# Order of partitions in three kinds of DMA of a four-stage convolution kernel, and its copies by way of DRAM cut into seven

## The chip, the core and the metric

One core of a Trainium2 chip runs the whole kernel. The metric is the device time of one launch in microseconds. The kernel before took 13218.9 us (median of 3 runs, 13193.93 to 13242.16).

## The reference

The input x is 16 images of 32 channels of 64 x 64. Four stages follow one another, each reading a normalised x and adding its result to x:

```
x = x + L0(gn(x))   # Winograd convolution 3x3, 32 -> 32 channels
x = x + L1(gn(x))   # offsets = prelu(conv3x3(x)); at 9 taps a pixel, sample x bilinearly at the tap + offset,
                    # out[o] = sum over taps and 4 channels of the group: w * sample
x = x + L2(gn(x))   # four 3x3 convolutions with weights +-scale, a 1x1 one, rounded to integers between
x = x + L3(gn(x))   # 3x3 convolution and |row difference| x W_edge, times a squeeze-and-excite gate
```

L1, the deformable convolution, is the costly one: each of the 9 taps of each of 4096 pixels is sampled at its own place.

## The kernel before, in words

**Layout.** An image is held as 128 partitions: 4 strips of 16 rows times 32 channels. The 16 images go through a software pipeline: in period n the kernel does for image n+1 stages L0, the offsets of L1 and their tables (the code's `a`), for image n the sampling and convolution of L1 (`b`), and for image n-1 stages L2 and L3 (`c`). A period has 24 slots (`SLOTS`); every engine runs through the same slots in the same order, with semaphores between them. There are 18 periods (-1 to 16), of which periods 0 to 15 hold the sampling.

**The sampling.** Six of the nine taps are fetched by GpSimd with indirect DMAs from a table in DRAM, 192 per image (L580). The other three, the dense taps, are computed. In each slot TensorE multiplies an image of 64 rows by 12 columns (twice, for two windows, so 128 partitions) by a matrix `select` that holds for each sample the weight of each row: 3 tiles `t` of 3 matmuls of 512 columns (L1328, two instructions each, so 18). VectorE multiplies each tile by the column weights `col_hat` (L1069), and TensorE sums the result with `w_dense` (L1340, `fold_dense`). `select` is made by ScalarE from `row_in` with an Abs (L630) and a Relu (L632).

**The dense loads.** For each slot, `row_in` and `col_hat` are each 128 partitions of 1536 numbers (768 KB), read from one row of a small table in DRAM, `coord_table`. `row_in` holds two different rows of 1536 numbers, each repeated for 64 partitions, and ScalarE's queue issues it (`load_rows`, L620). `col_hat` holds four, each repeated for 32 partitions, and SyncE issues it (`load_cols`, L437). Both are double buffered. In slot s ScalarE makes `select` for slot s+1 and then issues the load of `row_in` for slot s+2; SyncE issues `col_hat` for slot s+1 as soon as TensorE has folded slot s-1.

**The copies by way of DRAM.** The 3 x 3 convolutions want the image as 96 partitions: 3 horizontal shifts times 32 channels, whole rows. `store_plane` (L394) writes the 128 strip partitions to a plane of 32 channels in DRAM, and `load_taps` (L399) reads it back three times, shifted by one element. There are six such pairs per period: one for the offsets and five for L2 and L3. Each is placed in the slots so that the load is issued one slot after the store and the convolution comes one slot after the load.

**Order of SyncE's queue.** SyncE issues nearly all DMAs, in slot order, and each waits for its own semaphore first. The store of the image table, two times three DMAs in slots 18 and 19 (L457, L458, L460), stands in the same queue; so do the store of the coordinate table (L501, slot 21) and the load of the next image from it (L447). At the end of a period ScalarE's load of `row_in` for the next image (issued in slot 22) waits for the coordinate table, which VectorE computes in slot 21 (L1042 to L1053).

## Time and profile before

| | |
|---|---|
| runs, median (lowest to highest) | 13218.9 us (13193.93 to 13242.16) |
| profiled execution | 13156.62 us |
| its span | 13154.8 us |
| TensorE busy | 5385.4 us (41%), mean granted clock 0.679 |
| VectorE busy | 2994.6 us (23%) |
| ScalarE busy | 1772.0 us (13%) |
| GpSimd busy | 3027.3 us (23%) |
| DMA | 1049.75 MB, mean 80 GB/s, 16 engines |

The page's second part shows a flat picture over the whole span: TensorE 3 to 4 tenths, DMA 2 tenths, every engine idle more than half of the time. The chain of waits says what the span consists of; the share of busy time does not. A "slot" below is one step of the 24 of a period; in the middle of the trace a period takes about 793 us.

### The profile page before, as it was taken

To read this page: it belongs to the slowest core of one execution; us is meant where nothing else is said; L and a number is where in the kernel's file an instruction comes from. 1 tells how busy PE (TensorE), PEld (TensorE's weight loads), DVE (VectorE), ACT (ScalarE), POOL (GpSimd) and SP (SyncE) were. 2 spreads that over 40 slices of the span, in tenths; PEclk is the share of its full clock that TensorE was granted. 3 is DMA by queue.
4 is the path that set the end of the run, shared out by engine and by line. 5 is a ranking of instruction groups with operands and counts; after the bars stand their busy time and mean duration, and the time that the engine had idled before them with its cause. 6 is when DMAs were issued, how large, how long until landed. Compare 5 with 4: busy or idle time off the path is not lost.

```text
span 13154.8 us, 73595 instructions
## 1 busy us (share of the span) xinstructions
PE 5385.4 (41%) x24993; PEld 2557.4 (19%) x24993; DVE 2994.6 (23%) x5550; ACT 1772.0 (13%) x1990; POOL 3027.3 (23%) x3095
## 2 busy tenths in 40 slices
PE   2444344443444434434443434434344443344432
PEld 1222112121221212112121211211122121121110
DVE  2222122222222222222222222212222222222111
ACT  1111111111111111111111111111111111111110
POOL 2222132221222222122221322213222222222210
PEclk7666676666666666666666766666666666666665
DMA  3222222222222222222222222222222222222221
GB/s 86 74 85 76 73 92 77 82 81 77 86 77 92 79 80 83 77 85 80 88 76 74 91 77 84 80 75 87 76 88 79 81 79 78 90 78 80 80 74 37
DMA packets 447808, 1049.75 MB, mean 80 GB/s; under 512 B 237844, under 2 KB 274036, under 8 KB 438260
## 3 DMA queue, kind: packets, MB, share of 16 engines
q1 hardware_dynamic: 299252, 541.60, 12.8%
q10 hardware_dynamic: 49920, 301.99, 5.9%
q0 software_dynamic: 98304, 201.52, 5.7%
q8 instruction: 233, 3.82, 0.1%
q14 instruction: 99, 0.81, 0.0%
HBM read 943.72 MB, written 99.59 MB: 79 GB/s over the span
## 4 chain that ended last, share of the span: by engine, by line
DMA 71%; another core or an unknown queue 12%; SPq 8%; ACT 4%; DVE 1%; PE 1%; issue 1%; ACTq 0%; DVEq 0%
DMA row_in<-coord_table 64%; SPq L458 6%; ACT select L630 4%; DMA col_hat<-coord_table 3%; DMA plane_c<-xn_c 2%; SPq L460 1%; DMA coord_table<-wino 1%; PE ps_r L1328 1%; DMA taps_c<-plane_c 1%; DMA taps_c<-plane_act 0%; SPq L501 0%; DMA wino<-plane_a 0%; ACTq L620 0%; DVE wino L1048 0%
## 5 line engine op out<-in xcount | busy, mean ns | idle before, releaser
L580 POOL DMA_INDIRECT ring<-patch_table,idx_part x3072 | 3018.5, 983 | 9678.9 <-ACT idx_part L608 6132.5
L1328 PE MATMUL ps_r<-select,image 128*128 128x512 f32 x6912 | 3741.3, 696 | 2668.3 <-DVE col_hat L1069 1645.1
L1069 DVE TENSOR_TENSOR col_hat<-ps_r,col_hat 128x512 f32<-128x512 f32 x1152 | 794.9, 690 | 6990.5 <-PE ps_r L1328 4088.1
L1328 PEld LDWEIGHTS ps_r<-select,image 128*128 128x128 f32 x6912 | 1485.3, 225 | 4570.1 <-issue 2580.8
L630 ACT ACTIVATE select<-row_in,minus_row 128x1536 f32<-128x1536 f32 x384 | 604.6, 1575 | 10293.5 <-DMA row_in<-coord_table 10293.5
L1340 PE MATMUL ps_y<-col_hat,w_dense 128*32 128x128 f32 x9216 | 491.3, 362 | 914.1 <-ACT conv_out L656 903.5
L1354 PE MATMUL ps_t<-ident,values 128*128 128x128 f32 x1024 | 203.3, 333 | 1403.2 <-ACT samples L649 1403.1
L632 ACT ACTIVATE select<-select,one_col 128x1536 f32<-128x1536 f32 x384 | 604.6, 1574 | 12.5
L1340 PEld LDWEIGHTS ps_y<-col_hat,w_dense 128*32 128x32 f32 x9216 | 321.0, 144 | 1121.0 <-ACT conv_out L656 961.7
L1080 DVE TENSOR_TENSOR ring<-ring,w_cur 128x768 f32<-128x768 f32 x512 | 486.0, 949 | 17.6 <-DMA ring<-patch_table,idx_part 17.6
L1354 PEld LDWEIGHTS ps_t<-ident,values 128*128 128x128 f32 x1024 | 154.0, 174 | 1597.2 <-ACT samples L649 1486.5
L1271 PE MATMUL ps_a<-wino,w_freq 128*128 128x64 f32 x1152 | 218.2, 376 | 389.4 <-ACT wino L666 362.9
L1124 DVE TENSOR_SCALAR work_c<-work_c 128x1024 f32<-128x1024 f32 x64 | 44.4, 694 | 1262.6 <-ACT work_c L707 1262.2
L1314 PE MATMUL ps_c<-taps_c,w_edge_conv 96*32 96x512 f32 x768 | 134.2, 852 | 480.1 <-DMA taps_c<-plane_c 480.1
L1314 PE MATMUL ps_c<-taps_c,w_sign 96*32 96x512 f32 x768 | 125.8, 823 | 487.6 <-DMA taps_c<-plane_c 487.6
L1271 PEld LDWEIGHTS ps_a<-wino,w_freq 128*128 128x128 f32 x1152 | 217.5, 291 | 403.4 <-ACT wino L666 365.0
L1314 PE MATMUL ps_a<-wino,w_off 96*32 96x512 f32 x768 | 126.1, 825 | 409.6 <-DMA wino<-plane_a 409.6
L1084 DVE TENSOR_TENSOR ring<-ring 128x384 f32<-128x384 f32 x512 | 281.7, 550 | 4.4
L1314 PE MATMUL ps_c<-taps_c,w_signs 96*32 96x512 bf16 x1152 | 131.9, 627 | 316.4 <-DMA taps_c<-plane_act 316.4
L649 ACT COPY samples<-ps_t 128x512 f32<-128x512 f32 x256 | 147.6, 576 | 421.9 <-PE ps_t L1354 421.9
L1090 DVE TENSOR_TENSOR values<-ring 128x192 f32<-128x192 f32 x512 | 179.4, 350 | 4.5
L1282 PE MATMUL ps_a<-ident,wino_c 128*128 128x128 f32 x128 | 30.6, 418 | 316.6 <-ACT wino_c L684 316.6
(225 smaller groups left out, 2628.0 us busy)
## 6 DMA issues: line engine op xcount, KB each, us to landing
row_in<-coord_table ACTq DMA_DIRECT2D x384, 768.0 KB
col_hat<-coord_table SPq DMA_DIRECT2D x384, 768.0 KB
taps_c<-plane_c SPq DMA_DIRECT2D x32, 1608.8 KB
ring<-patch_table,idx_part POOLq DMA_INDIRECT x3072, 3.7
taps_c<-plane_act SPq DMA_DIRECT2D x48, 804.4 KB
wino<-plane_a SPq DMA_DIRECT2D x16, 1608.8 KB
plane_c<-xn_c SPq DMA_DIRECT2D x32, 520.0 KB
coord_table<-wino SPq DMA_DIRECT2D x64, 216.0 KB
```

The lines of the kernel that those rows point to most:

```text
L458: sp.dma_start(to[0:P - XW, lo:hi, 2 * C:], stage[XW:P, lo:hi]).then_inc(table_out, 16)
L580: nc.gpsimd.indirect_dma_start(out=ring[j][:, h % 2, k, :], out_offset=None, in_=table, in_offset=bass.IndirectOffsetOnAxis(ap=idx_part[:, ...
L630: nc.scalar.activation(sel, row_in[s % 2][:], ACT.Abs, bias=minus_row[:]).then_inc(row_in_read, 1)
L632: nc.scalar.activation(sel, sel, ACT.Relu, bias=one_col[:], scale=-1.0).then_inc(select_made, 1)
L1069: v.tensor_tensor(hat_t, ps_r[:, (s + t) % 2], hat_t, ALU.mult).then_inc(tile_weighed, 1)
L1080: return chain.add(v.tensor_tensor(tile, tile, wts, ALU.mult))
L1084: return chain.add(v.tensor_tensor(tile[:, :, 0:2 * C], tile[:, :, 0:2 * C], tile[:, :, 2 * C:], ALU.add))
L1271: ins = mm(ps_a[:, f % 2, b_ * NT:(b_ + 1) * NT], flat_w(w_freq, f * FREQ + b_), wino_v[:, f, :, b_, :], start=True, stop=True)
L1314: ins = mm(ps[s * C:(s + 1) * C, h], w[:, k0 + dy], src[:, r0:r0 + RS // 2, 0:W], start=(dy == 0), stop=(last and dy == 2))
L1328: ins = mm(ps_r[:, (s + t) % 2], image[:, m, t], select[s % 2][:, m], start=(m == 0), stop=(m == PAIRS - 1))
L1340: ins = mm(ps_y[j * C:(j + 1) * C, :], w_dense[:, DT - 1 - e].rearrange("p g o -> p (g o)"), col_hat[s % 2][:, t, j * P:(j + 1) * P], star ...
L1354: ins = nc.tensor.transpose(ps_t[:, j * P:(j + 1) * P], values[:, g % 2, j, 4 * k:4 * k + 4].rearrange("p k c -> p (k c)"), ident[:])
```

## The change

Four DMAs change their access patterns.

- `row_in`: the partitions are ordered as 64 image rows times 2 windows (partition = 2 x row + window) and no longer 2 x 64. The DRAM side of the load is then 64 (repeated) x 2 x 1536, not 2 x 64 (repeated) x 1536.
- `col_hat`: 32 x 4 instead of 4 x 32, in the same way.
- `store_plane`: four DMAs of 32 partitions instead of one whose pattern is 4 x 32.
- `load_taps`: three DMAs of 32 partitions instead of one whose pattern is 3 x 32.

All else follows from the new partition order: the image is loaded to every second partition, ScalarE's copy of it (`place_image`, three per period) reorders columns from (w, c) to (c, w), the weights `w_dense` get a mask of 16 partitions per group and a raw copy of their own, and `minus_row` is minus half the partition number, rounded. These last are done once, ahead of the loop. The counts that are waited for grow with the number of DMAs.

```diff
             def store_plane(dst, src, done):
-                sp.dma_start(dst.ap()[:, 1 + XW:1 + XW + STRIPS * RS * XW].rearrange("c (s x) -> s c x", s=STRIPS),
-                             src[:, 1 + XW:1 + XW + RS * XW]).then_inc(done, 16)
+                for s in range(STRIPS):
+                    sp.dma_start(dst.ap()[:, 1 + XW + s * RS * XW:1 + XW + (s + 1) * RS * XW],
+                                 src[s * C:(s + 1) * C, 1 + XW:1 + XW + RS * XW]).then_inc(done, 16)
             def load_taps(dst, plane, done):
-                sp.dma_start(dst, bass.AP(plane, 0, [[1, SHIFTS], [XG + 2, C], [1, XG]])).then_inc(done, 16)
+                for dx in range(SHIFTS):
+                    sp.dma_start(dst[dx * C:(dx + 1) * C, :], plane.ap()[:, dx:dx + XG]).then_inc(done, 16)
...
-                             part.rearrange("o (w x) -> (o w) x", w=WQ)[:, None, :].to_broadcast([WQ, C, WT * HALF])
+                             part.rearrange("o (w x) -> o w x", w=WQ).to_broadcast([C, WQ, WT * HALF])
                              ).then_inc(col_hat_in[s % 2], 16)
...
-                        sp.dma_start(image_next[h * H:(h + 1) * H, m * WIN * C:(m + 1) * WIN * C].rearrange(
+                        sp.dma_start(image_next[h:P:2, m * WIN * C:(m + 1) * WIN * C].rearrange(
...
-                    sp.wait_ge(plane_a_out, n * 16 + 16)
+                    sp.wait_ge(plane_a_out, n * PLANE_OUT + PLANE_OUT)
...
-                                    part.rearrange("o (h x) -> (o h) x", h=2)[:, None, :].to_broadcast([2, H, PAIRS * HALF])
+                                    part.rearrange("o (h x) -> o h x", h=2).to_broadcast([H, 2, PAIRS * HALF])
                                     ).then_inc(row_in_in[s % 2], 16)
...
-                new = image_next.rearrange("p (m t f) -> p m t f", m=PAIRS, t=WT)
+                new = image_next.rearrange("p (m t w c) -> p m t c w", m=PAIRS, t=WT, w=WQ)
...
-                    nc.scalar.copy(image[:, :, t], new[:, :, t]).then_inc(image_ready, 1)
+                    nc.scalar.copy(image[:, :, t].rearrange("p m (c w) -> p m c w", w=WQ), new[:, :, t]).then_inc(image_ready, 1)
...
-TAPS_IN = 16
+PLANE_OUT = STRIPS * 16
+TAPS_IN = SHIFTS * 16
```

On SyncE's queue, in slots 2 to 5 of the loop's body, before (`plane_c` and `plane_act` are the planes in DRAM, `xn_c` and `act_c` the strips, `taps_c` the 96 partitions; register instructions stand as ISA and REGISTER_ALU):

```order
L394 DMA plane_c<-xn_c 4x32x1040
L434 ISA
L437 ISA
L437 DMA col_hat<-coord_table 128x1x1536
L471 ISA
L399 DMA taps_c<-plane_c 96x1x4290
L434 ISA
L437 ISA
L437 DMA col_hat<-coord_table 128x1x1536
```

and now:

```order
L397 DMA plane_c<-xn_c 32x1040 x4
L439 ISA
L442 ISA
L442 DMA col_hat<-coord_table 128x1x1536
L476 ISA
L403 DMA taps_c<-plane_c 32x4290 x3
L439 ISA
L442 ISA
L442 DMA col_hat<-coord_table 128x1x1536
```

Nothing has changed its place: the store and the load of each copy stand where they stood, as four and three instructions in a row. The loads of `col_hat` (here) and of `row_in` (on ScalarE's queue) read word for word as before, since only the order inside their patterns differs. TensorE's order has no change but line numbers.

## Rows read from the trace of the kernel before

**Rows 1.** Page, part 4: shares of the chain that ended last, by line.
```profile
DMA row_in<-coord_table 64%; SPq L458 6%; ACT select L630 4%; DMA col_hat<-coord_table 3%; DMA plane_c<-xn_c 2%; SPq L460 1%; DMA coord_table<-wino 1%; PE ps_r L1328 1%; DMA taps_c<-plane_c 1%; DMA taps_c<-plane_act 0%; SPq L501 0%; DMA wino<-plane_a 0%; ACTq L620 0%; DVE wino L1048 0%
```
**Rows 2.** Waits: who waited for whom, us in total, times, longest.
```profile
ACT select L630 <- DMA row_in<-coord_table: 10293.5, 384, 62.3
...
DVE col_hat L1069 <- DMA col_hat<-coord_table: 2901.9, 128, 63.9
```
**Rows 3.** Chain of waits, mid-trace: start us, us, what.
```profile
6003.07 1.58 ACT select L630
...
6004.83 17.49 DMA row_in<-coord_table
...
6024.19 28.66 DMA row_in<-coord_table
```
**Rows 4.** Page, part 3: ScalarE's DMA queue; packets, MB, share of 16 engines.
```profile
q10 hardware_dynamic: 49920, 301.99, 5.9%
```
**Rows 5.** DMA issues with time to landing: whole trace, then 12890 to 13155 us.
```profile
patch_table<-values SPq DMA_DIRECT2D x1, 4224.0 KB, 16.8
...
out<-work_c SPq DMA_DIRECT2D x8, 128.0 KB, 2.2
```
**Rows 6.** Chain of waits at the start and in the last period.
```profile
85.50 39.67 DMA wino<-plane_a
...
12906.56 10.31 DMA plane_c<-xn_c
12916.89 40.32 DMA taps_c<-plane_c
...
12970.51 6.12 DMA plane_act<-act_c
12976.66 19.40 DMA taps_c<-plane_act
```
**Rows 7.** Timeline of SyncE, a store of the image table in mid-trace.
```profile
6381.74 52.37 SPq L458 DMA_DIRECT2D patch_table<-stage  x1
```
**Rows 8.** Page, part 5: the costliest groups on GpSimd and TensorE.
```profile
L580 POOL DMA_INDIRECT ring<-patch_table,idx_part x3072 | 3018.5, 983 | 9678.9 <-ACT idx_part L608 6132.5
L1328 PE MATMUL ps_r<-select,image 128*128 128x512 f32 x6912 | 3741.3, 696 | 2668.3 <-DVE col_hat L1069 1645.1
```
**Rows 9.** Windows: stretch, us, busy PE, PEld, DVE, ACT, POOL, PEclk, DMA share, GB/s.
```profile
5590.00:6383.00 793.00, 336.35 (x1562) 159.44 (x1562) 186.13 (x343) 108.85 (x124) 187.49 (x192) 0.68 0.25 81
...
5650.00:5700.00 50.00, 23.65 (x94) 10.39 (x94) 14.05 (x34) 3.40 (x3) 38.10 (x39) 0.73 0.45 129
...
6017.00:6029.00 12.00, 10.55 (x59) 4.48 (x52) 10.39 (x15) 3.86 (x5) 2.01 (x2) 0.93 0.15 43
...
12896.00:13155.00 259.00, 33.44 (x235) 11.55 (x233) 39.68 (x57) 15.32 (x24) 0.00 (x0) 0.54 0.12 34
```
**Rows 10.** Timeline of a slot that has its loads (start, us, engine, line).
```profile
6017.69 5.95 PE L1328 MATMUL ps_r<-select,image 128*128 128x512 f32 x12
...
6024.87 2.84 PE L1328 MATMUL ps_r<-select,image 128*128 128x512 f32 x6 [1.24 <-DVE col_hat L1069]
...
6027.65 0.64 PE L1340 MATMUL ps_y<-col_hat,w_dense 128*32 128x128 f32 x16
...
6028.86 5.42 PE L1328 MATMUL ps_r<-select,image 128*128 128x512 f32 x12
```
**Rows 11.** Timeline around slot 22, where the coordinate table is awaited.
```profile
6470.40 0.93 DVE L1042 TENSOR_SCALAR wino<-wino 96x128 f32<-96x128 f32 x6
6470.63 5.42 PE L1328 MATMUL ps_r<-select,image 128*128 128x512 f32 x12
...
6486.31 0.25 ACT L733 ACTIVATE hidden<-ps_c,b_att 4x1 f32<-4x1 f32 x1 [9.17 <-DMA coord_table<-wino]
```
**Rows 12.** Timeline of SyncE at the start: four DMAs of 32 partitions in a row.
```profile
2.58 1.81 SPq L384 DMA_DIRECT2D x<-x  x4
```
**Rows 13.** Lines L394 and L399: duration of an issue, ns, min/median/max.
```profile
L394 SPq DMA_DIRECT2D plane_c<-xn_c x32: 549/579/596, 1002.2 to 13085.3; - x32
...
L399 SPq DMA_DIRECT2D taps_c<-plane_c x32: 723/736/783, 1018.2 to 13095.6; - x32
```

More of the change, by code:

```diff
@@ L362, in build @@
         raw_d = raw_part(TAPS * 4)
+        raw_dense = raw_part(TAPS * 4)
         raw_2t = raw_part(CONVS * 3 * C)
@@ L370, in build @@
         prep_small = raw_part(32)
+        dense_mask = raw_part(8)
         n_weight_dmas = 0
@@ L423, in load_later @@
                 sp.dma_start(b_att1[:], batt1).then_inc(weights_in, 16)
+                sp.dma_start(raw_dense, w1d[:, None, :].to_broadcast([C, WQ, TAPS * 4])).then_inc(weights_in, 16)
                 sp.dma_start(raw_2t[0:TAPC, :], w2t).then_inc(weights_in, 16)
                 sp.dma_start(raw_3t[0:TAPC, :], w3t).then_inc(weights_in, 16)
-            n_weight_dmas = STRIPS * (len(later) + 1) + 3
+            n_weight_dmas = STRIPS * (len(later) + 1) + 4
             def load_cols(n, s):
@@ L470, in c_taps @@
                     i = at.index(s)
-                    sp.wait_ge(plane_c_out, n * (16 * len(at)) + 16 * (i + 1))
+                    sp.wait_ge(plane_c_out, n * (PLANE_OUT * len(at)) + PLANE_OUT * (i + 1))
                     if i in (0, len(at) - 1):
@@ L558, in _ @@
                                           channel_multiplier=1, allow_small_or_imprecise_dtypes=True))
-                chain.step(nc.gpsimd.iota(minus_row[ps], pattern=[[0, 1]], base=0, channel_multiplier=-1,
-                                          allow_small_or_imprecise_dtypes=True))
+            chain.step(nc.gpsimd.iota(minus_row[:], pattern=[[0, 1]], base=0, channel_multiplier=-1,
+                                      allow_small_or_imprecise_dtypes=True))
             chain.step(nc.gpsimd.memset(one_col[:], 1.0))
@@ L781, in prepare_rest @@
                 chain.step(v.tensor_scalar(group_mask[:], group_mask[:], float(STRIPS), None, ALU.mult))
+                chain.step(v.tensor_reduce(dense_mask, ident[:].rearrange("p (g i) -> p g i", i=4 * WQ), AX.X, ALU.add))
                 dve.wait_ge(weights_in, 16 * n_weight_dmas)
@@ L791, in prepare_rest @@
                     chain.add(v.tensor_scalar(w_dconv[:, :, g, :], by_chunk, group_mask[:, g:g + 1], None, ALU.mult))
-                    chain.add(v.tensor_scalar(w_dense[:, :, g, :], raw_d4[:, TAPS - DT:TAPS, :], group_mask[:, g:g + 1],
-                                              -1.0, ALU.mult, ALU.mult))
+                    chain.add(v.tensor_scalar(w_dense[:, :, g, :],
+                                              raw_dense.rearrange("p (k o) -> p k o", o=4)[:, TAPS - DT:TAPS, :],
+                                              dense_mask[:, g:g + 1], -1.0, ALU.mult, ALU.mult))
                 signs = raw_2t[0:TAPC, :]
@@ L1225, in _ @@
             dve.wait_ge(grid_ready, 1)
+            chain.step(v.tensor_scalar(minus_row[:], minus_row[:], 0.5, 0.25, ALU.mult, ALU.add))
+            chain.step(v.tensor_scalar(minus_row[:], minus_row[:], ROUND, ROUND, ALU.add, ALU.subtract))
             dve.wait_ge(zeroed, 4)
```

## The prediction

> **What bounds the kernel now.** I read the chain of waits first. Of the span, 64% is the flight of one load, `row_in` [rows 1], and no engine's work reaches 5%. The waits say the same from the engine's side: ScalarE stands 10293.5 us before its Abs for that load, 384 times of 384 [rows 2], 26.8 us each on average; VectorE waits a further 2901.9 us for `col_hat`. The reader should see in the chain how it closes on itself [rows 3]: the Abs of slot s+1 starts, 1.6 us later the load for slot s+2 is issued, and the next Abs starts when that lands. Only one load is in flight at a time, so a slot can't be shorter than load + 1.8 us. The shortest flights are 17.49 us, most are 28 to 40, when other transfers sit on the same DMA engines.
>
> How fast is the load? Its queue moved 301.99 MB in 5.9% of 16 engines' span [rows 4], that is 0.059 x 16 x 13154.8 = 12418 us of engine time, 24.3 GB/s for an engine while it works. One load is 786432 bytes, so 32.4 us of engine time. It lands in 17.49 us at best: that is two engines (16.2 us) and 1.3 us around them. Two is the outermost dimension of its pattern (2 x 64). The copies, with 3 and 4 outside, are slow as well: in the last period nothing else is in flight, and yet the taps take 40.32 us (1608.8 KB, even less than 3 x 24.3 GB/s) and the plane's store 10.31 us [rows 6], while a store of 32 partitions (128 KB) lands in 2.2 us with three more beside it, and a write of 4224 KB whose outermost dimension is 128 in 16.8 us, 257 GB/s [rows 5]. That is more than ten engines at 24.3 GB/s. I read from it that the outermost dimension sets how many engines work, and take all 16 for 32, 64 and 128. So the DMA engines are not full (25% in a period [rows 9]); the kernel waits for the two or three of them that get the work.
>
> The Trainium skill, "DMA: Bandwidth & Descriptors", section "Why a DMA increments its semaphore by 16 and not by 1", says that a DMA is spread over the largest number up to 16 that divides the slowest dimension of both its sides. By that rule the new patterns (64 or 32 outside, 128 or 32 partitions) all get 16 engines; the trace agrees on the two of `row_in`, and no row shows a repeated source with 16.
>
> **The change, part by part.**
>
> *`row_in` and `col_hat`.* With 16 engines a load needs 32.4 / 16 = 2.0 us of transport and 1.3 us around it: 3.3 us at best. `col_hat` is issued at about the same time and uses the same engines, and the gathers too, so I take 5 to 6 us. Bound from above: all 16 engines now read the same 12 KB of DRAM, which no row shows; the fastest 50 us of the trace moved 129 GB/s [rows 9], and at that rate both loads together take 12.2 us. The closed chain then gives 1.8 + 5.5, about 7.5 us a slot (at worst 14). It is 33 us now (793 / 24).
>
> *What is late next.* TensorE. In a slot that has its loads [rows 10] the 18 instructions on the image start 0.43 us apart at full clock, 7.7 us; then VectorE must weigh the third tile before the last fold, and the next slot starts 1.4 us after the last matmul's step: 9.1 us for a slot with nothing else in it. That is above 7.5. I add up TensorE's path over a period:
> - matmuls on the image: 6912 / 16 = 432 x 0.43 = 186 us [rows 8, 10];
> - TensorE's other work: (5385.4 - 3741.3) / 16 = 103 us at the mixed clock of now; 95 us when more of it runs at full clock;
> - the idle moment at each slot's end, 0.4 us x 24 = 10 us;
> - slots where another engine is late. The end of a period is the largest: VectorE starts the coordinates at 6470.40, and ScalarE's next work, behind the wait for their table, comes at 6486.31 [rows 11], while TensorE began that slot at 6470.63 and needs its result before it may fold. The slot becomes 18 us instead of 9, so 9 us, none of it shortened by the change. Behind the heavy VectorE slots (5, 8, 9, 21), where it has 5 to 8 us of L0, L2 and offset work after the third tile and TensorE only allows about 4.5, I count 1 to 4 us each, 17 us in all. Together 26 us;
> - clock and late loads: the granted clock is 0.93 in a stretch where TensorE is busy 10.55 of 12 us and 0.68 over a period where it is busy 42% [rows 9]. I expect it nearly always at 2.4 GHz (level 1.0), and at 1.2 GHz for about a tenth of the image matmuls after a stall: 19 us. Loads that come late behind taps or table stores: 22 us, with nothing but judgement behind it; bounds 0 and 24 x 4 = 96.
>
> Sum: 186 + 95 + 10 + 26 + 41 = 358 us a period against 796 (the middle part of the trace, 163 to 12896 us, is 16 periods).
>
> *The seven DMAs.* Per period there are six stores and six loads, so 6 x 3 + 6 x 2 = 30 DMAs more. They cost SyncE 18 x 0.58 + 12 x 0.74 = 19 us a period of issue [rows 13]; SyncE has nothing to compute, and each copy has one to two slots (15 to 30 us) before it is used. One copy: four issues 2.3 us, 520 KB at 257 GB/s 2.1, around it 1.3: 5.7 us instead of 10.3; the taps three issues 2.2 us, 1608.8 KB 6.4, 1.3: about 9 us (10 if the issues are not overlapped) instead of 40.3. In bf16 5 instead of 6.1 and 6.7 instead of 19.4. Inside a period they are hidden behind TensorE's slots. Queued behind them on SyncE are the loads of `col_hat`, whose slack is a slot of TensorE minus their 5 us; that is where cover may be thin. SyncE's stall at the table store, 52.37 us [rows 7], comes, as I read it, from a DMA queue that is full behind the taps; it should go to the few us that the transfers need.
>
> The Trainium skill speaks against this part: in the same page, "Rules for kernel authors", small transfers are to be merged into one large one, and "Anatomy of one DMA" puts about 2 us of fixed cost on each. If the extra 30 each took 2 us in a row, a period would be 60 us longer, 960 us in all. The trace has four DMAs of 32 partitions issued in 1.81 us [rows 12], and those of the output landing in 2.2 us, so the fixed parts overlap, and I keep only the issue time.
>
> *Ends.* Start: 163 us up to the first `row_in`; the taps' 39.67 us [rows 6] go to 9 and the store saves 5, so 127. Last period: 259 us [rows 9], minus 2 x 31.3 and 3 x 12.9 for taps, 2 x 4.8 and 3 x 1.1 for stores: 145.
>
> *ScalarE's strided copy of the image, the longer setup, two more tiny VectorE instructions:* three copies a period, now 0.5 us; if the order (c, w) doubled them, 1.5 x 16 = 24 us; setup under 5 us. Not counted, in the range.
>
> **The sum.** 16 x 358 + 127 + 145 = 6000 us, against the profiled execution's 13156.62 (span 13154.8). The median of the runs lies 0.5% above that execution, so 6030; I say 6000.
>
> **Rivals.**
> 1. *Transport stays the bound.* 1049.75 MB over 384 slots is 2.73 MB a slot. The 257 GB/s is one lone contiguous write; sources repeated from one small place, small pieces, and reads and writes mixed may give much less, and with engines waiting for one another at the same DRAM or the same partitions the whole may stay near 129 GB/s. Then a slot takes 21 us, and the kernel 384 x 21.2 + 272 = 8400 us. For it: nothing in the trace is both wide and repeated. Against it: two engines reading one place side by side keep 24.3 GB/s each, and 129 was reached without pressure. 7000 to 9500 us.
> 2. *GpSimd's gathers.* 3072 x (0.983 + 0.30) = 3940 us, 246 a period, 31 us for every three slots [rows 8]. The three lightest slots take 31 us too. If denser VectorE work slows each gather's issue by a third, a period comes to about 410 us: 6850 us.
> 3. *The change doesn't do what it says.* If the number of engines hangs on something else than the outermost dimension, both loads keep two and four engines, and the time stays at 13200. Against it stands 17.49 us, which fits two so well.
> 4. *Slower.* One mechanism: 16 engines hammer the same 12 KB of DRAM, and each read queues behind fifteen others. It decides from the point where `row_in` takes over 27 us, which is 16 engines together below 29 GB/s, less than the 45 that two reach now (786432 / 17.49 us). A load of 30 us gives 13.2 + 0.384 x 3 ms, some 14400 us.
>
> **Chances.** Forecast 0.73 (its own range 5500 to 6900), transport 0.17, gathers 0.05, no effect 0.03, slower 0.02. The range that should hold 8 in 10: below, a period of 320 us (no late loads, full clock, VectorE's slots better hidden) gives 5400; above, the 96 us of late loads plus gathers, or the lower part of rival 1, give 7500. A measurement of this kernel tells 0.3% from no change. Faster by more than that 0.95, within 0.03 (rival 3), slower 0.02.
>
> **What would show it.** Right: Abs waits for `row_in` under 6 us in most slots and the chain of waits runs through TensorE, VectorE and the coordinates' table; periods near 358 us; taps of the last period near 9 us; granted clock above 0.9; L458 a few us; DMA near 170 GB/s. Wrong: `row_in` still heads the chain with more than 10 us of flight (rival 1); GpSimd's share above 75% with VectorE waiting for `ring` (rival 2); flights of 17 us unchanged (rival 3). The weakest term is the 41 us of clock and late loads, then the 17 us behind VectorE; each hangs on how the engines' small delays add up.

## The result, and the profile after

The changed kernel takes 5254.25 us (median of 4 runs, 5238.0 to 5263.32) against 13213.41 us: ratio 0.3974, 95% interval 0.3961 to 0.3988. The forecast was 6000 us, with a range of 5400 to 7500. The direction and the cause were right; the time lies 12% below the forecast and 3% below the range. The numbers below are of the profiled execution, with a span of 5261.5 us.

From the page's first four parts: busy time by engine, the granted clock in 40 slices, ScalarE's DMA queue, and the shares of the chain of waits by engine and by line.

```profile
PE 4408.5 (84%) x24993; PEld 2077.6 (39%) x24993; DVE 2987.9 (57%) x5553; ACT 1793.4 (34%) x1990; POOL 3259.5 (62%) x3094
...
PEclk8999989899999999999899899999999999899995
...
q10 hardware_dynamic: 55296, 302.01, 17.2%
...
PE 50%; DMA 22%; DVE 14%; SPq 7%; issue 4%; ACT 2%; ACTq 0%; POOL 0%; DVEq 0%; another core or an unknown queue 0%; POOLq 0%
PE ps_r L1339 33%; DMA taps_c<-plane_c 8%; PE ps_c L1325 6%; DMA wino<-plane_a 4%; DMA plane_a<-xn_a 3%; DMA plane_c<-xn_c 3%; PE ps_a L1282 3%; PE ps_a L1325 2%; PE ps_y L1351 2%; DMA col_hat<-coord_table 2%; SPq L397 2%; DVE col_hat L1077 2%; PE ps_t L1365 1%; SPq L403 1%; SPq L506 1%
```

`row_in` had 64% of the chain of waits [rows 1]; it is no longer among the lines named. TensorE has half of it. DMAs still have 22%, and most of that is the copies. The queue of `row_in` moved the same bytes in 0.172 x 16 x 5261.5 = 14480 us of engine time, so 20.9 GB/s an engine where it was 24.3 [rows 4], 14% less. Sixteen engines on one 12 KB source do not get in one another's way by more than that; how much of the 14% is the shared source, and how much the other transfers that now run beside it, isn't shown.

The number of engines can be read off the packets. A load of `row_in` has 128 packets of 6144 bytes, one for each partition. Before, the queue had 49920 packets [rows 4], 384 x (128 + 2); now it has 55296, 384 x (128 + 16). The trace has the rest as packets of 4 bytes: two a load before and sixteen now, which fits one for each engine at the end of its share. In the last period of the kernel before, the load of taps has three of them and the store of a plane four; now each of the seven DMAs has sixteen.

The waits (engine, line, for whom; us in total, times, longest):

```profile
ACT select L635 <- DMA row_in<-coord_table: 924.9, 143, 22.9
...
DVE col_hat L1077 <- DMA col_hat<-coord_table: 373.4, 55, 14.9
ACT hidden L738 <- DMA coord_table<-wino: 195.7, 14, 14.1
PE ps_c L1325 <- DMA taps_c<-plane_c: 195.0, 32, 17.0
...
PE ps_r L1339 <- DVE col_hat L1077: 153.2, 114, 9.1
PE ps_a L1325 <- DMA wino<-plane_a: 131.5, 16, 14.8
PE ps_c L1418 <- ACT hidden L738: 92.8, 15, 6.7
```

ScalarE's wait for `row_in` fell from 10293.5 to 924.9 us, VectorE's for `col_hat` from 2901.9 to 373.4 [rows 2]. What TensorE itself waits for is now the thing to read, and it is short. The first load of `row_in`, where the forecast's start ends, is issued at 125.58 us:

```profile
125.58 0.66 ACTq L625 DMA_DIRECT2D row_in<-coord_table  x1
```

A slot with nothing but its loads, from the timeline:

```profile
2343.94 7.99 PE L1339 MATMUL ps_r<-select,image 128*128 128x512 f32 x18
...
2346.52 0.57 ACTq L625 DMA_DIRECT2D row_in<-coord_table  x1
...
2353.08 5.42 PE L1339 MATMUL ps_r<-select,image 128*128 128x512 f32 x12
2353.16 1.58 ACT L635 ACTIVATE select<-row_in,minus_row 128x1536 f32<-128x1536 f32 x1 [4.86 <-DMA row_in<-coord_table]
```

The next slot's matmuls begin 9.14 us after this one's: the 9.1 us of the forecast [rows 10]. `row_in` is issued at 2346.52 and its Abs starts at 2353.16, 6.6 us later (17.49 at best before [rows 3]); `select` is double buffered, so TensorE does not feel that. Four stretches of the span (columns as in [rows 9]):

```profile
150.80:418.00 267.20, 247.24 (x1372) 120.38 (x1372) 149.30 (x288) 99.37 (x104) 206.55 (x200) 0.96 0.67 212
418.00:4857.00 4439.00, 3846.17 (x21868) 1808.80 (x21868) 2598.08 (x4800) 1560.57 (x1733) 2850.66 (x2688) 0.94 0.69 206
4857.00:5123.50 266.50, 247.23 (x1343) 111.69 (x1344) 135.42 (x219) 95.79 (x98) 166.32 (x159) 0.96 0.65 204
5123.50:5261.50 138.00, 36.30 (x238) 12.38 (x236) 39.70 (x57) 15.32 (x24) 0.00 (x0) 0.58 0.27 64
```

The first stretch and the third are the first and the last period with sampling, and take 267 us each; the 14 between them take 4439 / 14 = 317 us each. The fourth is the rest of the kernel. The granted clock is 0.94 where it was 0.68 [rows 9], DMA moves 206 GB/s and not 81.

The end of the kernel, from the chain of waits:

```profile
5136.67 2.21 DMA plane_c<-xn_c
5139.70 9.36 DMA taps_c<-plane_c
...
5164.27 1.73 DMA plane_act<-act_c
5166.82 4.68 DMA taps_c<-plane_act
```

These are the flights of the last DMA of each group, counted from its own issue: 9.36 us for the taps instead of 40.32, in bf16 4.68 instead of 19.40, the stores 2.21 instead of 10.31 and 1.73 instead of 6.12 [rows 6]. In the middle of the trace the taps are slower, and TensorE waits for them:

```profile
2674.33 12.50 DMA taps_c<-plane_c
...
2817.36 13.81 DMA wino<-plane_a
```

One such place on TensorE, slot 15, where the offsets' convolution awaits its taps, and the two windows around it:

```profile
2513.38 8.37 PE L1325 MATMUL ps_a<-wino,w_off 96*32 96x512 f32 x48 [10.15 <-DMA wino<-plane_a]
```

```profile
2503.40:2513.30 9.90, 0.00 (x0) 0.00 (x0) 5.47 (x7) 0.00 (x0) 7.91 (x7) 0.62 1.02 228
2513.40:2518.50 5.10, 5.10 (x24) 1.17 (x28) 0.00 (x0) 3.15 (x2) 3.88 (x5) 0.50 0.65 188
2522.40:2530.20 7.80, 7.80 (x22) 3.45 (x20) 2.71 (x4) 0.12 (x1) 0.94 (x1) 1.00 0.38 118
```

While TensorE stands still the DMA engines are full (share 1.02, 228 GB/s): taps, `row_in` and `col_hat` are in flight at once. Behind the wait the first matmuls run at a granted clock of 0.50, the lower level of 1.2 GHz, and only then at 1.00. A wait costs itself and some us more. I add it up from the matmuls' groups (busy us, mean ns, idle before them):

```profile
L1339 PE MATMUL ps_r<-select,image 128*128 128x512 f32 x6912 | 3205.4, 612 | 208.9 <-DVE col_hat L1077 153.2 <-ACT image L646 50.7 <-issue 1.8
...
L1325 PE MATMUL ps_c<-taps_c,w_sign 96*32 96x512 f32 x768 | 128.1, 836 | 125.7 <-DMA taps_c<-plane_c 125.7
L1325 PE MATMUL ps_a<-wino,w_off 96*32 96x512 f32 x768 | 127.8, 835 | 131.5 <-DMA wino<-plane_a 131.5
L1325 PE MATMUL ps_c<-taps_c,w_edge_conv 96*32 96x512 f32 x768 | 118.7, 764 | 69.2 <-DMA taps_c<-plane_c 69.2
...
L1325 PE MATMUL ps_c<-taps_c,w_signs 96*32 96x512 bf16 x1152 | 75.7, 399 | 48.9 <-DMA taps_c<-plane_act 48.9
```

TensorE waits 125.7 + 131.5 + 69.2 + 48.9 = 375.3 us for copies.

### The profile page after: what moved, and what is told of

It is laid out like the page before. It is cut to its first block, busy times and chain, and to the rows that moved or that the text cites. A ratio compares the mean times of both kernels' runs of the same rounds, so it can differ in the third digit from the quotient of the medians.

```text
span 5261.5 us, 74078 instructions
## 1 busy us (share of the span) xinstructions
PE 4408.5 (84%) x24993; PEld 2077.6 (39%) x24993; DVE 2987.9 (57%) x5553; ACT 1793.4 (34%) x1990; POOL 3259.5 (62%) x3094
## 3 DMA queue, kind: packets, MB, share of 16 engines
q10 hardware_dynamic: 55296, 302.01, 17.2%
## 4 chain that ended last, share of the span: by engine, by line
PE 50%; DMA 22%; DVE 14%; SPq 7%; issue 4%; ACT 2%; ACTq 0%; POOL 0%; DVEq 0%; another core or an unknown queue 0%; POOLq 0%
PE ps_r L1339 33%; DMA taps_c<-plane_c 8%; PE ps_c L1325 6%; DMA wino<-plane_a 4%; DMA plane_a<-xn_a 3%; DMA plane_c<-xn_c 3%; PE ps_a L1282 3%; PE ps_a L1325 2%; PE ps_y L1351 2%; DMA col_hat<-coord_table 2%; SPq L397 2%; DVE col_hat L1077 2%; PE ps_t L1365 1%; SPq L403 1%; SPq L506 1%
## 5 line engine op out<-in xcount | busy, mean ns | idle before, releaser
L585 POOL DMA_INDIRECT ring<-patch_table,idx_part x3072 | 3250.8, 1058 | 1810.2 <-issue 1588.7
L1339 PE MATMUL ps_r<-select,image 128*128 128x512 f32 x6912 | 3205.4, 612 | 208.9 <-DVE col_hat L1077 153.2
L1339 PEld LDWEIGHTS ps_r<-select,image 128*128 128x128 f32 x6912 | 1285.4, 194 | 1791.4 <-issue 1496.7
L635 ACT ACTIVATE select<-row_in,minus_row 128x1536 f32<-128x1536 f32 x384 | 605.0, 1575 | 1642.3 <-DMA row_in<-coord_table 924.9
L1351 PE MATMUL ps_y<-col_hat,w_dense 128*32 128x128 f32 x9216 | 367.6, 283 | 23.6 <-DVE col_hat L1077 17.6
L1351 PEld LDWEIGHTS ps_y<-col_hat,w_dense 128*32 128x32 f32 x9216 | 230.1, 111 | 198.1 <-issue 122.4
L1325 PE MATMUL ps_a<-wino,w_off 96*32 96x512 f32 x768 | 127.8, 835 | 131.5 <-DMA wino<-plane_a 131.5
L1325 PE MATMUL ps_c<-taps_c,w_sign 96*32 96x512 f32 x768 | 128.1, 836 | 125.7 <-DMA taps_c<-plane_c 125.7
L1325 PE MATMUL ps_c<-taps_c,w_edge_conv 96*32 96x512 f32 x768 | 118.7, 764 | 69.2 <-DMA taps_c<-plane_c 69.2
L1282 PE MATMUL ps_a<-wino,w_freq 128*128 128x64 f32 x1152 | 139.5, 283 | 26.3 <-DVE wino L892 26.3
L1365 PE MATMUL ps_t<-ident,values 128*128 128x128 f32 x1024 | 153.6, 273 | 0.0
L1282 PEld LDWEIGHTS ps_a<-wino,w_freq 128*128 128x128 f32 x1152 | 139.6, 201 | 33.6 <-DVE wino L892 26.4
L712 ACT ACTIVATE work_c<-ps_c,bn_bias,bn_scale 128x512 f32<-128x512 f32 x160 | 115.4, 771 | 70.6 <-PE ps_c L1325 70.1
L671 ACT COPY wino<-ps_a 128x384 f32<-128x384 f32 x96 | 45.9, 478 | 212.9 <-PE ps_a L1282 212.9
```

What stands on the lines that cost most here:

```text
L585: nc.gpsimd.indirect_dma_start(out=ring[j][:, h % 2, k, :], out_offset=None, in_=table, in_offset=bass.IndirectOffsetOnAxis(ap=idx_part[:, ...
L635: nc.scalar.activation(sel, row_in[s % 2][:], ACT.Abs, bias=minus_row[:]).then_inc(row_in_read, 1)
L1282: ins = mm(ps_a[:, f % 2, b_ * NT:(b_ + 1) * NT], flat_w(w_freq, f * FREQ + b_), wino_v[:, f, :, b_, :], start=True, stop=True)
L1325: ins = mm(ps[s * C:(s + 1) * C, h], w[:, k0 + dy], src[:, r0:r0 + RS // 2, 0:W], start=(dy == 0), stop=(last and dy == 2))
L1339: ins = mm(ps_r[:, (s + t) % 2], image[:, m, t], select[s % 2][:, m], start=(m == 0), stop=(m == PAIRS - 1))
L1351: ins = mm(ps_y[j * C:(j + 1) * C, :], w_dense[:, DT - 1 - e].rearrange("p g o -> p (g o)"), col_hat[s % 2][:, t, j * P:(j + 1) * P], star ...
```

## The experiments

All ratios are to the kernel before, with their 95% interval. Each diff is an excerpt. The time of a slot is the distance between the first image matmul of one slot and of the next, median over the first 15 periods with sampling of a trace.

### The parts apart

`row_only`: the order and the load of `row_in` alone, on the kernel before.

```diff
-   part.rearrange("o (h x) -> (o h) x", h=2)[:, None, :].to_broadcast([2, H, PAIRS * HALF])
+   part.rearrange("o (h x) -> o h x", h=2).to_broadcast([H, 2, PAIRS * HALF])
```

> Of the change only the new order of row_in (64 x 2 outside) and what follows from it; col_hat (4 outside) and the copies (4 and 3 outside) as before. If the outermost dimension sets the number of DMA engines, row_in's flight falls below 10 us, but the lowest three engines still carry all taps and a quarter of col_hat: per period 2.5 MB of taps, 4.7 MB of col_hat, 0.6 MB of stores and about 2 MB of their share of the rest each, near 10 MB at 24.3 GB/s, some 400 to 480 us a period, so 7000 to 8500 us in all, with col_hat and the taps at the head of the waits. Rival, that one closed chain through row_in was all that bound the kernel: under 6000 us.

Measured: 8444.52 us, ratio 0.639 (0.635 to 0.6431), at the upper end of the range. The next wait is the one that the double buffer had hidden; the page's shares of the chain by line:

```profile
DMA col_hat<-coord_table 27%; PE ps_r L1331 11%; DMA taps_c<-plane_c 10%; DMA wino<-plane_a 7%; DMA plane_a<-xn_a 7%; SPq L458 6%; DMA plane_c<-xn_c 5%; DMA plane_act<-act_c 3%; PE ps_c L1317 2%; DMA taps_c<-plane_act 2%; PE ps_a L1317 1%; DVE col_hat L1069 1%; PE ps_a L1274 1%; SPq L447 1%; SPq L501 1%
```

`copies_only`: the seven DMAs alone.

```diff
-   sp.dma_start(dst, bass.AP(plane, 0, [[1, SHIFTS], [XG + 2, C], [1, XG]])).then_inc(done, 16)
+   for dx in range(SHIFTS):
+       sp.dma_start(dst[dx * C:(dx + 1) * C, :], plane.ap()[:, dx:dx + XG]).then_inc(done, 16)
```

> Only the copies in seven DMAs; both dense loads as before. Two engines carry 24 x 393 KB of row_in and 24 x 197 KB of col_hat a period and their share of the rest, about 15.5 MB, 640 us at 24.3 GB/s: 10000 to 11500 us by the theory of engine counts, the chain still headed by row_in. If the copies matter only at start and end of the launch: 13213 - 145 = 13070 us.

Measured: 11906.09 us, 0.901 (0.8953 to 0.9067), above the 10000 to 11500 us of the theory of engine counts, and far below the 13070 of its rival. The copies' gain shows although `row_in` bounds each slot; as I read it, taps and stores on three or four engines were in the way of the two that its load uses. The gain was overrated, and why isn't shown.

`no_row`: `col_hat` and the copies changed, the order and the load of `row_in` as before.

```diff
-   part.rearrange("o (h x) -> o h x", h=2).to_broadcast([H, 2, PAIRS * HALF])
+   part.rearrange("o (h x) -> (o h) x", h=2)[:, None, :].to_broadcast([2, H, PAIRS * HALF])
```

> All of the change but the new order of row_in. Its flight cannot be under 17.5 us (two engines), so the closed chain gives at least 24 x 19.3 = 463 us a period and, with the sixteenths of all other transfers on the same two engines, about 530: 8000 to 9300 us. Rival, all loads share one capacity and the order of row_in alone does little: under 6500 us.

Measured: 10127.82 us, 0.7664 (0.7616 to 0.7712), above my range: with everything else out of the way `row_in` still holds the kernel at 10128 / 384 = 26 us a slot, and has 87% of the chain of waits.

`dense_only`: both dense loads changed, the copies as before, one DMA each.

```diff
-   for dx in range(SHIFTS):
-       sp.dma_start(dst[dx * C:(dx + 1) * C, :], plane.ap()[:, dx:dx + XG]).then_inc(done, 16)
+   sp.dma_start(dst, bass.AP(plane, 0, [[1, SHIFTS], [XG + 2, C], [1, XG]])).then_inc(done, 16)
```

> row_in and col_hat in the new order, the copies by way of DRAM as single DMAs as before. If the copies are exposed where a convolution waits for them: flights of taps of 30 to 45 us instead of 12, in three slots of a period (4, 15, 20) about 25 us more each, a few more behind the three smaller ones and SyncE's table store stalling again: period 318 + 80 to 120 us, 6400 to 7300 us in all. Rival, the prediction's step that the copies lie hidden behind TensorE's slots: only start and last period longer, about 5254 + 145 = 5400 us.

Measured: 7714.81 us, 0.5838 (0.5802 to 0.5875), above the 6400 to 7300 us expected and 2461 us above the changed kernel. TensorE waits for the copies:

```profile
PE ps_c L1323 <- DMA taps_c<-plane_c: 1083.0, 32, 54.5
PE ps_c L1323 <- DMA taps_c<-plane_act: 853.0, 48, 32.7
PE ps_a L1323 <- DMA wino<-plane_a: 574.7, 16, 53.1
```

That is 2511 us against 375 in the changed kernel, and 2136 of the 2450 us between the two spans. The store of the image table shows the full queue again, once behind taps and once (26 us earlier) not, in the timeline of SyncE:

```profile
2239.80 2.80 SPq L461 DMA_DIRECT2D patch_table<-stage  x1
...
2263.73 0.78 SPq L401 DMA_DIRECT2D taps_c<-plane_c  x1
...
2265.36 39.42 SPq L461 DMA_DIRECT2D patch_table<-stage  x1
```

So the 52.37 us [rows 7] were the taps on three engines, as read. The parts don't add: the copies are worth 1307 us alone and 2461 us behind the dense loads; `row_in` is worth 4769 us alone and 4873 us at the end.

### Is it the order of the partitions or the number of engines?

`old_order_split`: the old order of partitions everywhere; `row_in` by 2 DMAs of 64 partitions, `col_hat` by 4 of 32, the copies in seven. Every DMA then has 64 or 32 outermost, too.

```diff
+   for h in range(2):
+       nc.scalar.dma_start(row_in[s % 2][h * H:(h + 1) * H].rearrange("p m x -> p (m x)"),
+                           part[:, h * PAIRS * HALF:(h + 1) * PAIRS * HALF].to_broadcast([H, PAIRS * HALF])
+                           ).then_inc(row_in_in[s % 2], 16)
```

> The partitions in the order of before, but row_in loaded by two DMAs of 64 partitions and col_hat by four of 32, each with its own row as a source; the copies in seven. If only the number that stands outermost in each DMA matters (64 and 32, so all 16 engines), this is as fast as the changed kernel, 5200 to 5350 us, and 384 x 4 more DMAs cost only issue time on queues that have room. Rival: the new order of the partitions, by which neighbours hold different rows, does something of its own (for the DRAM row or the partitions' ports): more than 2% off, either way.

Measured: 5606.2 us, 0.4249 (0.4235 to 0.4262), 6.7% above the changed kernel, so the rival came true. Of the 7959 us gained, 7607 come with any pattern of 32 or 64 outside, and 352 only with the changed kernel's own DMAs. Three ways to lose those 352: one DRAM row read at a time, 64 neighbouring partitions written at a time, or the issue of four more DMAs a slot. For the first two, the next runs take the new order and cut `row_in` in two, first into partitions 0 to 63 and 64 to 127 (both rows in each), then into even and odd ones (one row each).

```diff
+   for h in range(2):
+       nc.scalar.dma_start(row_in[s % 2][h * H:(h + 1) * H].rearrange("p m x -> p (m x)"),
+                           part.rearrange("o (h x) -> o h x", h=2).to_broadcast([H // 2, 2, PAIRS * HALF])
```

```diff
+   for h in range(2):
+       nc.scalar.dma_start(row_in[s % 2][h:P:2].rearrange("p m x -> p (m x)"),
+                           part[:, h * PAIRS * HALF:(h + 1) * PAIRS * HALF].to_broadcast([H, PAIRS * HALF])
```

> The changed kernel with row_in loaded by two DMAs, partitions 0 to 63 and 64 to 127; each still reads two rows in turn (pattern 32 x 2). In the run with the old order and split loads the row_in queue's engines worked at 14.0 GB/s instead of 20.9. If the cause is that one DMA wrote only half of the partitions (two engines at one door to them), this one has the same fault: near 14 to 16 GB/s, and a time between 5254 and 5450 us (col_hat stays as in the changed kernel). If the cause is that all engines read one row of DRAM at a time, this reads two and keeps 20 to 21 GB/s: under 5290 us.

> The changed kernel with row_in loaded by two DMAs, even and odd partitions, so each is spread over all partitions but reads one row of DRAM 64 times. Half of the partitions as the cause: 20 to 21 GB/s kept, under 5290 us. One row of DRAM at a time as the cause: near 14 to 16 GB/s and up to 5450 us. (Against the run before, exactly one of these two should keep its rate.)

Measured: halves 5411.9 us, 0.4092 (0.4074 to 0.4111); evens 5287.44 us, 0.3998 (0.3982 to 0.4015). The queue of `row_in` in the page of the halves, then of the evens:

```profile
q10 hardware_dynamic: 61440, 302.04, 24.0%
```

```profile
q10 hardware_dynamic: 61440, 302.04, 17.2%
```

With spans of 5419.0 and 5282.8 us an engine moves 14.5 GB/s in halves and 20.8 in evens; in one piece it was 20.9. Both use all 16 engines: 61440 packets are 384 x (128 + 2 x 16). So neighbouring partitions slow the engines, a single source row does not. The evens are 0.6% (33 us) slower than the changed kernel, with intervals that overlap, so a second DMA for each `row_in` costs little or nothing. The halves lose 158 us of the 352. The other 194 probably belong to `col_hat`, cut into four DMAs of 32 neighbouring partitions; whether by their place or by their number wasn't tested.

### What the transport still costs

`small_rows` loads 16 of `row_in`'s 1536 numbers from the second image on, `small_taps` 130 of 4290 elements of two of the three f32 taps. Both leave most of a transfer out and keep its place and its waits.

```diff
+   row_in[s % 2][:, 0, 0:16], part.rearrange("o (h x) -> o h x", h=2)[:, :, 0:16].to_broadcast([H, 2, 16])
```

```diff
+   load_taps(taps_c[:], plane_c, taps_c_in, 2 * XW)
```

> Left out: from the second image on row_in's loads fetch 16 of 1536 numbers per partition (the rest is stale), so half of the dense traffic, 18 MB a period, is gone. If the dense loads no longer bound the kernel (my term of 22 us a period for late loads was too large by nearly all of it), this gains only a few us a period where the taps' flights get shorter: 5080 to 5240 us. If transport still set the pace (rival 1 of the prediction), a third of the bytes less would take the time below 4900.

> Left out: the two float32 loads of taps for L2 and L3 fetch 130 of 4290 numbers per row (the rest is stale). If slots 4 and 20 wait for these flights (11 and 6 us a period in the trace of the changed kernel), a period falls by 14 to 20 us and the last period by 14: 4900 to 5030 us. If the waits are taken over by another engine that was only just hidden, under 100 us are gained.

Measured: 5052.05 us, 0.3826 (0.3814 to 0.3838), and 5006.52 us, 0.3791 (0.3779 to 0.3803). The first gains more than I expected (5080 to 5240) and stays far from the 4900 of rival 1, the second lies in its range. The rows' 4% are not gained where the rows are awaited: the light slots stay at 9.1 us, slot 4 goes from 25.4 to 19.4 us and slot 15 from 28.4 to 22.7. As I read it, the `row_in` load is in the way of the copies, on the same engines. With small taps slot 4 takes 14.4 us and slot 20 17.9 instead of 23.6.

### Can the copies' waits be ordered away?

`both_late`: the load of the next image moved behind the offsets' plane store, and the load of `row_in` for the next image behind L3's work in slot 22.

```diff
-                if live(n + (s + 2) // SLOTS):
+                if live(n + (s + 2) // SLOTS) and s != 22:
...
+                if live(n + (s + 2) // SLOTS) and s == 22:
+                    load_rows(n + (s + 2) // SLOTS, (s + 2) % SLOTS)
```

> The changed kernel with two moves. SyncE issues the next image's four loads behind the store of plane_a and not ahead of it; ScalarE issues the first row_in of the next image behind its work for L3 in slot 22 and not ahead of it. Theory: the taps of slot 15 arrive 3 to 5 us earlier, and TensorE no longer stands 8 us in slot 22, of which 3 to 6 come back in slots 23 and 0, where select is late instead: 5 to 10 us a period, 5100 to 5180 us. Rival: both waits only move, within 0.5% of 5254.

Measured: 5285.26 us, 0.3999 (0.3985 to 0.4012). That is 0.6% above the changed kernel. My theory fell: slot 22 lost 7.4 us and slot 23 gained 9.7.

`convs_late`: on TensorE three convolutions one slot later (the offsets' from 15 to 16, L2's first from 4 to 5, the edges' from 20 to 21), so that each copy has a slot more.

```diff
-                if s == 15:
+                if s == 16:
...
-                if s == 4:
+                if s == 5:
...
-                if s == 20:
+                if s == 21:
```

> The changed kernel with three convolutions one slot later on TensorE: the offsets' from slot 15 to 16, the first of L2 from 4 to 5, that of L3 from 20 to 21. If TensorE's waits for taps are only lateness (11, 14 and 6 us a period), the flights are covered by one more slot and about 25 us a period go, less 2 to 5 us where the next step now waits for ScalarE within the same slot: 4820 to 4930 us. Rival: the whole chain of L2 moves with it and the waits come back at its later convolutions: over 5100 us.

Measured: 5153.33 us, 0.3898 (0.3886 to 0.391), 1.9% below the changed kernel, about a quarter of what I expected. The rival's time came true (over 5100), but not its mechanism: L2's later convolutions wait 50.0 us for their bf16 taps, as before (48.9). The page's groups say where the rest went:

```profile
L1339 PE MATMUL ps_r<-select,image 128*128 128x512 f32 x6912 | 3287.7, 625 | 478.7 <-DVE col_hat L1077 423.3 <-ACT image L646 50.9 <-issue 1.8
...
L1325 PE MATMUL ps_a<-wino,w_off 96*32 96x512 f32 x768 | 89.8, 617 | 15.1 <-DMA wino<-plane_a 15.1
L1325 PE MATMUL ps_c<-taps_c,w_sign 96*32 96x512 f32 x768 | 87.5, 604 | 14.7 <-DMA taps_c<-plane_c 14.7
```

The waits of TensorE for copies fell from 375 to 96 us, the wait for the gate's `hidden` from 93 to 0, and the three f32 convolutions now run at the higher clock (from 374.6 to 269.0 us busy): 477 us in all. Against it the wait for `col_hat` rose from 153 to 423 us, and the image matmuls behind that wait now run at the lower clock (82 us more): 352 us back. That leaves 125, and the spans differ by 118.

`reordered`: the same, and the coordinates (ScalarE's copy, VectorE's arithmetic, the store) in slot 20 instead of 21. `coords_early`: the coordinates alone. `convs45_coords`: the coordinates and the convolutions of slots 15 and 4, but not the edges'.

```diff
-                if s == 21:
+                if s == 20:
```

> As convs_late, and the coordinates' table one slot earlier (ScalarE's copy, VectorE's 24 instructions and SyncE's stores from slot 21 to 20). TensorE stands about 9 us in slot 22 and 5 in slot 23 for what follows from this table; a slot of 9 us earlier should take 8 to 12 us a period off: 4650 to 4800 us. Rival: VectorE is the late one in slots 20 and 21 and nothing is gained against convs_late.

> Only the coordinates (ScalarE's copy, VectorE's arithmetic, the store) in slot 20 instead of 21; all convolutions as in the changed kernel. Theory 1 (the end of a period costs what the coordinates' chain costs, and the wait for the edge taps in slot 20 covers it): slot 22 falls from 18.4 to about 9.1, the rest stays, slots 20 to 23 sum to about 57 us, the period loses 9 and the time is 5254 - 14 x 9 = about 5130 us (5110 to 5170). Theory 2 (as both late loads showed, a wait at the end of a period only moves): slots 20 to 23 stay near 67 us, time 5235 to 5270.

> Only two of the three convolutions one slot later (offsets' 15 to 16, L2's first 4 to 5); the edge convolution stays in slot 20, and the coordinates' copy, arithmetic and store come in slot 20. In the changed kernel slots 20 to 23 take 23.6, 9.1, 18.4 and 15.6 us (67); with the edge convolution and the coordinates moved 10.4, 28.5, 9.1 and 13.6 (62). Theory 1: what was lost in slot 21 is the edge convolution's wait, squeezed behind VectorE's coordinates and a late col_hat; left in slot 20 it waits 14 us for its taps, and the coordinates are computed in that wait. Then slots 20 to 23 take about 24, 9.1, 9.1 and 14 = 56 us, the period 298 us instead of 304, and the time 5088 - 14 x 6 = about 5005 us (4970 to 5050). Theory 2: the coordinates in slot 20 delay col_hat or the squeeze wherever the edge convolution stands; slots 20 to 23 sum to 61 us or more again and the time is 5075 us or above.

Measured: `reordered` 5088.23 us, 0.3855 (0.3843 to 0.3868); `coords_early` 5123.29 us, 0.3876 (0.3862 to 0.389); `convs45_coords` 5036.46 us, 0.3812 (0.3794 to 0.3829). The first missed its range, as it was built on the same belief as `convs_late`. The last two came out as theory 1 had it: slots 20 to 23 take 23.1 + 9.1 + 10.8 + 13.5 and 24.2 + 9.1 + 9.1 + 13.6 us, so 56 to 57, and 67 in the changed kernel. The wait for the edges' taps is a cover for the coordinates; moved away, it leaves them bare. `convs45_coords` is the fastest kernel here that computes everything, 4.1% below the changed one.

In it one can see how a wait moves. Around the same taps as above, in its timeline and windows:

```profile
2431.50 0.69 DVE L1077 TENSOR_TENSOR col_hat<-ps_r,col_hat 128x512 f32<-128x512 f32 x1 [7.73 <-DMA col_hat<-coord_table]
...
2432.25 5.49 PE L1339 MATMUL ps_r<-select,image 128*128 128x512 f32 x6 [7.50 <-DVE col_hat L1077]
...
2437.67 5.36 PE L1325 MATMUL ps_a<-wino,w_off 96*32 96x512 f32 x48
```

```profile
2419.70:2431.50 11.80, 5.05 (x12) 1.90 (x10) 3.93 (x5) 2.53 (x2) 9.06 (x10) 0.83 0.99 284
...
2432.30:2437.60 5.30, 5.30 (x6) 1.80 (x6) 1.82 (x3) 0.00 (x0) 4.31 (x4) 0.50 0.35 107
```

The convolution no longer waits (10.15 us before) and takes 5.36 us instead of 8.37. But `col_hat`, issued behind the taps on SyncE's queue and carried by the same full engines (0.99, 284 GB/s), is 7.7 us late, TensorE waits 7.50 us at its third tile, and six image matmuls pay the low clock. Slots 15 and 16 sum to 36.6 us; they were 38.0.

## Why the forecast was right, and where it was wrong

| | forecast | measured |
|---|---|---|
| start, up to the first issue of `row_in` | 127 | 126 |
| from there to the first image matmul | not in the sum | 25 |
| 16 periods | 16 x 358 = 5728 | 14 x 317 + 267 + 267 = 4973 |
| last period's rest | 145 | 138 |
| sum | 6000 | 5262 |

**Right: the cause.** Two engines for 2 outside, three and four for the copies, sixteen now, as the packets say. `row_only`, `no_row` and `dense_only` show each group's part, `old_order_split` that 96% of the gain needs no new order of the partitions. Rival 3 (no effect) and rival 4 (one hot place in DRAM) are out: `split_evens` reads one row at a time and keeps the 20.8 GB/s of the other.

**Right: the closed chain and its successor.** A light slot takes 9.1 us, as worked out; VectorE, ScalarE and GpSimd don't bound it. Rival 2 came to a gather of 1058 ns instead of 983 [rows 8], not a third more. (Its price of 410 us a period doesn't follow from its terms: 192 gathers of 1.33 x 983 + 300 ns are 309 us.) Rival 1 (129 GB/s) is out with 206 GB/s over the middle; `small_rows` and `small_taps` show that transport is still felt, at 4 to 5%, at the copies.

**Right in size: a lone copy, SyncE's stall, the cost of more DMAs.** In the last period, from the first issue of a group to its last landing, the taps take 10.2 us (forecast 9, or 10), in bf16 5.5 (6.7), the stores 3.5 (5.7) and 3.0 (5). The store of the image table takes a median of 3.3 us (13.2 at most) instead of up to 52. ScalarE's copies of the image went from 509 to 847 ns, 16 us in all, inside the 24 that I had left out of the sum. By the Trainium skill, "DMA: Bandwidth & Descriptors", sections "Rules for kernel authors" and "Anatomy of one DMA", seven DMAs would by the prediction's estimate have been 960 us slower than two, if their fixed parts had come in a row. `dense_only` shows that two are 2461 us slower than seven. The 2 us of that second section stand there for DMAs that GpSimd issues, and these are SyncE's.

**Wrong: the period, 358 us instead of 317.** The steps of the prediction that failed are three terms of its sum, TensorE's other work (95 us, measured 75), the idle time (58 us, measured 42) and 16 full periods where two are 50 us shorter, and its statement on the copies that "inside a period they are hidden". One by one:
- *The first and the last period.* I took all 16 as full. They take 267 us each, 50 less than those between, which makes 100 of the 755 us by which the periods were off; the other 655 are 41 in each of the 16. The first has no L2 and L3 and the last no next image. The trace of the kernel before could have told me: its first period and the 14 between, in windows cut at the same matmuls, were

```profile
190.30:915.80 725.50, 312.65 (x1372) 153.60 (x1372) 149.44 (x288) 98.44 (x104) 204.24 (x211) 0.68 0.25 80
915.80:12170.60 11254.80, 4700.07 (x21870) 2229.87 (x21871) 2606.01 (x4802) 1543.42 (x1737) 2643.90 (x2688) 0.68 0.25 81
```

  so 725.5 us against 11254.8 / 14 = 803.9, and the last was 725.4. They were shorter even with `row_in` as the bound.
- *TensorE's other work, 95 us forecast, 75 measured* ((4408.5 - 3205.4) / 16). It was 103 at the mixed clock, and I let it shrink by 8% only. The large groups of it that aren't behind a wait shrank by a quarter or more (the folds of the dense taps, before):

```profile
L1340 PE MATMUL ps_y<-col_hat,w_dense 128*32 128x128 f32 x9216 | 491.3, 362 | 914.1 <-ACT conv_out L656 903.5 <-DVE col_hat L1069 7.5
```

  and after:

```profile
L1351 PE MATMUL ps_y<-col_hat,w_dense 128*32 128x128 f32 x9216 | 367.6, 283 | 23.6 <-DVE col_hat L1077 17.6 <-issue 0.6
```

  The f32 convolutions, which follow a wait, stayed as they were (mean 836 and 835 ns). This term is 20 us a period, half of the 41 by which the 14 middle ones were off; the image matmuls make 5 and the idle time 16, as follows.
- *The 19 us of low clock on the image matmuls* were nearly right: 3205.4 / 16 = 200 us against 186 + 19.
- *The idle time, 58 us forecast, 42.4 measured* (4439 - 3846.17, over 14), is right only as a sum. I had 10 at the slots' ends, 26 behind VectorE and the coordinates, 22 for late loads, and none for the copies. In the light slots no load is late. The rows have for each period: copies 19 (375.3 less the 92.7 us that `reordered` keeps, where they lie ahead of the first or behind the last period, over 15), `col_hat` 10, the gate behind the coordinates 6, the image's copy 3.
- *"Inside a period they are hidden", with "one to two slots (15 to 30 us)"*, is the step that failed outright. The same text has 9.1 us for a slot. The taps above, whose issue begins at 2673.50, are wanted by TensorE at 2679.68 (its matmuls start at 2686.87 after 7.19 us of waiting), 6.2 us later; the last flight takes 12.50 us beside the other loads, not the 9.36 of an empty chip. The copies cost 19 us of waiting and (374.6 - 269.0) / 15 = 7 of low clock a period.

So the forecast's largest error was on one side (busy time, other idle time and short periods), and an error of 26 us a period on the other side hid a third of it. That was luck. The start itself was right; the 25 us from the first issue of `row_in` to the first image matmul were in no term (27 in the kernel before, 163 to 190).

**The end of a period.** Slot 22 takes 18.3 us, the 18 of the forecast. ScalarE's wait for the table, behind which the gate stands, from the timeline:

```profile
2613.73 0.25 ACT L738 ACTIVATE hidden<-ps_c,b_att 4x1 f32<-4x1 f32 x1 [13.95 <-DMA coord_table<-wino]
2614.03 0.58 PE L1418 MATMUL ps_c<-hidden,w_att 4*128 4x1 f32 x2 [6.51 <-ACT hidden L738]
```

TensorE may fold only behind it and stands 6.51 us, as the forecast had it for before [rows 11]. What this place is worth was shown by `coords_early`: 131 us, 2.5%.

## What to carry to other kernels

When a stall goes, measure every cover again with the new, shorter slot: a transfer that is hidden by "a slot" of 33 us isn't by one of 9. Price work that ran at a low granted clock anew, except what stays behind a wait, and count the iterations that do less than a full one. Before moving a consumer later, ask what is queued behind its load on the same queue and the same DMA engines, since the wait may just go there; and leave a wait where other work lies in its shade.

## What the runs showed of the hardware

- A DMA to 64 neighbouring partitions runs its engines at 14.5 GB/s each (14.0 in `old_order_split`: 302.04 MB, 24.1% of 16 x 5605.2 us), one to 64 partitions two apart at 20.8, to all 128 at 20.9. Why neighbouring ones are slower isn't shown.
- A DMA whose pattern had 2, 3 or 4 outside ran on 2, 3 or 4 engines, one with 32 or 64 outside on 16: a load of `row_in` has 2 packets of 4 bytes beside its 128 of data before, and 16 after.
- Sixteen engines that read the same 12 KB of DRAM kept 86% of the rate that two of them had (20.9 against 24.3 GB/s), with 206 GB/s in all and not 81. The company counts too: in `row_only`, where taps and `col_hat` still crowd a few engines, it was 17.8 (302.01 MB, 12.6% of 16 x 8438.4 us).
- A wait of TensorE of 7.5 and of 10.15 us left it at 0.50, the level of 1.2 GHz, and cost a further 2.7 us on six image matmuls (5.49 against 2.84) and 3.0 us on a convolution (8.37 against 5.36).
